# Turning the head stacks of Q and K two heads at a time, with the third part written by a DMA within SBUF

## The reference

```python
x = x + 0.5 * ffn(_layernorm(x), w_gate, w_up, w_down)
x = x + attn(_layernorm(x), w_qkv, w_out, q_gain)
x = x + 0.5 * ffn(_layernorm(x), w_gate, w_up, w_down)

def ffn(x, w_gate, w_up, w_down):        # hidden size 2048
    return (silu(x @ w_gate.T) * (x @ w_up.T)) @ w_down.T

def attn(x, w_qkv, w_out, q_gain):
    q, k, v = split(x @ w_qkv)           # 16 heads of 32
    q, k = unit_norm(q), unit_norm(k)    # t * rsqrt(sum(t * t) + 1e-6)
    q, k = rope(q), rope(k)              # in every second head
    logits = (q @ k.T) * q_gain          # causal mask
    return (softmax(logits) @ v) @ w_out
```

## Time and profile before

| | |
|---|---|
| median of 3 runs | 2797.44 us (2796.15 to 2797.51) |
| the profiled execution | 2798.85 us |
| its span, first to last instruction | 2797.1 us |
| mean granted clock of PE | 0.994 |
| PE busy | 2726.2 us (97%) |
| DVE busy | 1780.7 us (64%) |
| ACT busy | 1205.0 us (43%) |
| POOL busy | 531.2 us (19%) |

### The profile page before, as it was taken

The page is one execution under the profiler, slowest core; times in us unless marked ns, Lnnn a source line. Parts: engine busy times, 40 slices in busy tenths (PEclk is TensorE's granted clock), DMA queues, the critical chain, the costliest instruction groups (busy, mean ns, idle before and its releaser), DMA issues.

```text
span 2797.1 us, 56089 instructions
## 1 busy us (share of the span) xinstructions
PE 2726.2 (97%) x22720; PEld 1992.9 (71%) x22720; DVE 1780.7 (64%) x5054; ACT 1205.0 (43%) x2250; POOL 531.2 (19%) x820
## 2 busy tenths in 40 slices
PE   4999999999999999999999999999999999999999
PEld 4677766777767777777767777677777776777776
DVE  7766666666656565666656666565666767676643
ACT  5443544354434434443434445344443444454422
POOL 0012132213130302213121121312203131313100
PEclk8999999999999999999999999999999999999999
DMA  7000000000000000000000000000000000000000
GB/s 257 1 16 1 16 1 1 1 17 16 2 1 16 16 2 1 1 16 16 2 1 9 9 16 1 1 16 9 8 5 13 16 2 1 1 16 9 2 9 16
DMA packets 16577, 39.37 MB, mean 14 GB/s; under 512 B 1472, under 2 KB 1472, under 8 KB 15808
## 3 DMA queue, kind: packets, MB, share of 16 engines
q1 hardware_dynamic: 16320, 35.79, 3.6%
HBM read 26.35 MB, written 9.44 MB: 13 GB/s over the span
## 4 chain that ended last, share of the span: by engine, by line
PE 87%; DVE 8%; issue 3%; ACT 2%; DMA 0%; POOL 0%; SPq 0%; DVEq 0%; ACTq 0%
PE psum L1045 25%; PE psum L1046 25%; PE psum L1047 25%; PE psum L1200 2%; PE psum L1176 2%; PE psum L1212 2%; PE psum L1068 1%; PE psum L1154 1%; PE psum L1158 1%; DVE arena L885 1%; DVE arena L883 1%; DVE arena L960 1%; PE psum L1213 1%; DVE arena L889 1%; ACT arena L775 1%
## 5 line engine op out<-in xcount | busy, mean ns | idle before, releaser
L1045 PE MATMUL psum<-arena,WG 128*128 128x256 f16 x2048 | 558.8, 273 | 4.9 <-DVE arena L885 3.4
L1045 PE MATMUL psum<-arena,WU 128*128 128x256 f16 x2048 | 558.9, 273 | 0.0
L1047 PE MATMUL psum<-arena,WG 128*128 128x256 f16 x2048 | 558.7, 273 | 0.0
L1047 PE MATMUL psum<-arena,WU 128*128 128x256 f16 x2048 | 558.5, 273 | 0.0
L1046 PE MATMUL psum<-arena,WU 128*128 128x256 f16 x2048 | 558.5, 273 | 0.0
L1046 PE MATMUL psum<-arena,WG 128*128 128x256 f16 x2048 | 558.5, 273 | 0.0
L883 DVE SCALAR_TENSOR_TENSOR arena<-arena,psum 128x256 f32<-128x256 f32 x512 | 214.8, 420 | 446.2 <-ACT arena L775 445.2
L775 ACT ACTIVATE arena<-psum,tscale 128x256 f32<-128x256 f32 x512 | 241.1, 471 | 564.4 <-PE psum L1047 563.7
L1045 PE MATMUL psum<-WD,arena 128*128 128x512 f16 x1024 | 388.8, 380 | 3.6 <-DVE arena L889 3.5
L1047 PE MATMUL psum<-WD,arena 128*128 128x512 f16 x1024 | 388.4, 379 | 0.0
L1046 PE MATMUL psum<-WD,arena 128*128 128x512 f16 x1024 | 388.4, 379 | 0.0
(11 more groups left out here) (145 smaller groups left out, 4465.2 us busy)
## 6 DMA issues: line engine op xcount, KB each, us to landing
arena<-in_L_attn_x SPq DMA_DIRECT2D x16, 512.0 KB, 3.7
out<-arena SPq DMA_DIRECT2D x16, 512.0 KB, 2.8
arena<-in_L_ffn_w_gate SPq DMA_DIRECT2D x4, 1024.0 KB, 9.2
arena<-in_L_ffn_w_up SPq DMA_DIRECT2D x4, 1024.0 KB, 7.3
WD<-in_L_ffn_w_down SPq DMA_DIRECT2D x4, 1024.0 KB, 12.5
arena<-in_L_attn_w_qkv SPq DMA_DIRECT2D x1, 3072.0 KB, 22.2
arena<-in_L_attn_w_out SPq DMA_DIRECT2D x1, 1024.0 KB, 6.7
park<-arena SPq DMA_DIRECT2D x2, 512.0 KB, 2.8
```

The source lines that it names most:

```text
L1045: T_.matmul(o, lhs(0), rhs(0), start=first, stop=False)
L1047: return T_.matmul(o, lhs(1), rhs(0), start=False, stop=last)
```

## The change

The stacks of Q and K are laid out as two parts for each head, 64 columns, in place of three: high, low for Q and low, high for K. The parts of two heads are then 128 adjacent columns, and one transpose turns them (`stk`, four for Q and four for K in place of eight and eight). The even head comes out on partitions 0 to 63 of PSUM, the odd one on 64 to 127 (`turned_pair`). ACT and DVE bring each with an own copy to partitions 0 to 63 of `QT` and `KT`. The third part, partitions 64 to 95, equals the first of Q (high) and the second of K (high), and SP copies it within SBUF with one DMA each (`stack_high`), which waits for the copy of this tile. The first score product of a half batch waits for the DMAs (`qt_dup`, `kt_dup`) in place of the copies. ACT writes all high parts of a tile in one activation where there were three. The order has a new stage "stack high" and a new `fill` "dup" behind the last tile, and shares of both tables are set anew.

```diff
@@ -103,7 +103,10 @@
     qn = [words("work", 2 * D + D * i, D) for i in range(2)]
     ropeU = words("work", 4 * D, D // 2)
     ropeV = words("work", 4 * D + D // 2, D // 2)
-    STK = halves("work", 5 * D, HH * ST).rearrange("p (h c) -> p h c", h=2 * HH)
+
+    stk = halves("work", 5 * D, (2 * D + 2 * HD) // 2)
+    STQ, STK = (stk[:, D * a:D * (a + 1)].rearrange("p (h c) -> p h c", h=HH) for a in range(2))
+    SThi = stk.rearrange("p (a c) -> p a c", a=2)[:, :, 0:D].rearrange("p a (h c) -> p a h c", c=2 * HD)[:, :, :, 0:HD]
 
     fH = [words("ffn", TH * i, TH) for i in range(2)]
     HP = [[halves("ffn", 2 * TH + TH * q + TH // 2 * i, TH // 2) for q in range(2)] for i in range(2)]
@@ -171,6 +174,10 @@
     def ps16(b):
         return psum[:, b * 512:(b + 1) * 512].bitcast(F16)
 
+    def turned_pair(bank, odd):
+
+        return ps16(bank)[2 * HD * odd:2 * HD * (odd + 1), 0:D].rearrange("p (h n) -> p h n", n=P)
+
     def wd_bank(m):
         return (0, 1, 2, 6, 7)[m % 5]
 
@@ -185,7 +192,7 @@
         dn_tr dn_st gmax_in gmax_all scales wd_hi wd_lo sel_done pro_hi pro_lo dve_pro pool_pro
         x_in0 x_in1 stored0 stored1 x1_done x2_done out_ready var_ready rstd_ready xn_done xt_ps xt_hi xt_lo
         qk_ps v_ps qs_done sq_done vhi_done vlo_done ssq_ready r_ready qn_done rope_done
-        st_hi st_lo qt_ps kt_ps qt_ev kt_ev s1_ps smax_done mst_done mt_ps mt_copied mrow_done
+        st_hi st_lo qt_ps kt_ps qt_ev kt_ev qt_dup kt_dup s1_ps smax_done mst_done mt_ps mt_copied mrow_done
         s2_ps exp_done cut_done phi_done plo_done pv_ps y_read ynorm_done yt_ps yt_hi yt_lo op_ps
         gu_ps tanh_done a_done gated h_hi h_lo down_done dve_chain pool_chain"""
     s = {n: nc.alloc_semaphore(n) for n in names.split()}
@@ -346,9 +353,10 @@
                 if t:
                     put(("stack", b, hf, t - 1))
                     fill(w["stack"])
-                    bank3(("stack turn", b, hf, t - 1), ("stack out", b, hf, t - 1))
+                    bank3(("stack turn", b, hf, t - 1), ("stack out", b, hf, t - 1), ("stack high", b, hf, t - 1))
                 else:
                     fill(w["v first"])
+            fill(w["dup"])
             fill(w["turned"])
 
         def maxima(b, hf, h, w):
@@ -471,12 +479,14 @@
 
     LOAD, LEFT, PACE = 9, 3, (0, 2, 3, 4)
     SHORT = (0, 1, 6, 7)
-    MANY = {"qk": 1.88, "qk first": 1, "ends": 3, "stack": 2, "v first": 1.25, "turned": 1, "max first": 0.4,
+    MANY = {"qk": 1.32, "qk first": 1, "ends": 1.92, "stack": 2, "v first": 1.25, "turned": 1, "max first": 0.4,
             "maxima": 1, "max rows": 1, "scores": 1, "exp": 1.5, "high": 1, "low": 1, "max": 1,
-            "head": 1, "end": 1, "end values": 0.5, "out 0": 1, "out 1": 2, "out 2": 1, "out 3": 1}
-    FEW = {"qk": 1, "qk first": 2, "ends": 2.4, "stack": 2, "v first": 1, "turned": 1, "max first": 0.32,
-           "maxima": 1, "max rows": 1, "scores": 0.8, "exp": 1.2, "high": 0.8, "low": 0.8, "max": 0.56,
-           "head": 0.56, "end": 0.8, "end values": 1, "out 0": 1.25, "out 1": 1.25, "out 2": 1, "out 3": 1.5}
+            "head": 1, "end": 1, "end values": 0.5, "out 0": 1, "out 1": 2, "out 2": 1.5, "out 3": 1,
+            "dup": 3}
+    FEW = {"qk": 1, "qk first": 2, "ends": 2.4, "stack": 2, "v first": 1.5, "turned": 1, "max first": 0.32,
+           "maxima": 1, "max rows": 0.8, "scores": 0.8, "exp": 1.2, "high": 0.8, "low": 0.8, "max": 0.56,
+           "head": 0.56, "end": 0.8, "end values": 1, "out 0": 1.25, "out 1": 1.25, "out 2": 1, "out 3": 1.5,
+           "dup": 3}
     ORDER = order()
     norms = [stage[1:] for stage in ORDER if stage[0] == "norm"]
     place_of_norm = {norm: k for k, norm in enumerate(norms)}
@@ -580,7 +590,15 @@
                 p, half = at
                 sp.dma_start(X[p][:, 2 * half:2 * half + 2, :], of).then_inc(s[loaded(what)[0]], 16)
 
-            run({"store": store, "load": load})
+            def stack_high(b, hf, t):
+
+                c = slice(t * P, (t + 1) * P)
+                sp.wait_ge(s["qt_ev"], tile_no(b, hf, t) + 1)
+                sp.dma_start(QT[2 * HD:ST, :, c], QT[0:HD, :, c]).then_inc(s["qt_dup"], 16)
+                sp.wait_ge(s["kt_ev"], tile_no(b, hf, t) + 1)
+                sp.dma_start(KT[2 * HD:ST, :, c], KT[HD:2 * HD, :, c]).then_inc(s["kt_dup"], 16)
+
+            run({"store": store, "load": load, "stack high": stack_high})
             for th in range(2):
                 sp.wait_ge(s[f"stored{th}"], 16 * len(STORES[th]))
 
@@ -736,14 +754,13 @@
                 if t:
                     act.wait_ge(s["kt_ps"], i)
                 q3 = qn[t % 2].rearrange("p (h c) -> p h c", c=HD)
-                nc.scalar.activation(STK[:, :, 0:HD], q3, ACT.Copy)
-                nc.scalar.activation(STK[:, 0:HH, HD:2 * HD], q3[:, 0:HH, :], ACT.Copy)
-                nc.scalar.activation(STK[:, HH:2 * HH, 2 * HD:ST], q3[:, HH:2 * HH, :], ACT.Copy).then_inc(s["st_hi"], 1)
+                nc.scalar.activation(SThi, q3.rearrange("p (a h) c -> p a h c", a=2), ACT.Copy).then_inc(s["st_hi"], 1)
 
             def stack_out(b, hf, t):
                 act.wait_ge(s["qt_ps"], tile_no(b, hf, t) + 1)
-                nc.scalar.activation(QT[0:ST, :, t * P:(t + 1) * P], ps16(2)[0:ST, :].rearrange("p (h n) -> p h n", h=HH),
-                                     ACT.Copy).then_inc(s["qt_ev"], 1)
+                for odd in range(2):
+                    ins = nc.scalar.activation(QT[0:2 * HD, odd::2, t * P:(t + 1) * P], turned_pair(2, odd), ACT.Copy)
+                ins.then_inc(s["qt_ev"], 1)
 
             def max_rows(b, hf, g):
                 act.wait_ge(s["mt_ps"], group_no(b, hf, g) + 1)
@@ -919,12 +936,14 @@
             def stack(b, hf, t):
                 dve.wait_ge(s["st_hi"], tile_no(b, hf, t) + 1)
                 q3 = qn[t % 2].rearrange("p (h c) -> p h c", c=HD)
-                V_.tensor_tensor(STK[:, 0:HH, 2 * HD:ST], q3[:, 0:HH, :], STK[:, 0:HH, 0:HD], ALU.subtract)
-                V_.tensor_tensor(STK[:, HH:2 * HH, HD:2 * HD], q3[:, HH:2 * HH, :], STK[:, HH:2 * HH, 0:HD], ALU.subtract).then_inc(s["st_lo"], 1)
+                V_.tensor_tensor(STQ[:, :, HD:2 * HD], q3[:, 0:HH, :], STQ[:, :, 0:HD], ALU.subtract)
+                V_.tensor_tensor(STK[:, :, 0:HD], q3[:, HH:2 * HH, :], STK[:, :, HD:2 * HD], ALU.subtract).then_inc(s["st_lo"], 1)
 
             def stack_out(b, hf, t):
                 dve.wait_ge(s["kt_ps"], tile_no(b, hf, t) + 1)
-                V_.tensor_copy(KT[0:ST, :, t * P:(t + 1) * P], ps16(3)[0:ST, :].rearrange("p (h n) -> p h n", h=HH)).then_inc(s["kt_ev"], 1)
+                for odd in range(2):
+                    ins = V_.tensor_copy(KT[0:2 * HD, odd::2, t * P:(t + 1) * P], turned_pair(3, odd))
+                ins.then_inc(s["kt_ev"], 1)
 
             mnegv = mneg[:, :].rearrange("p (t h) -> p t h", t=TT)
             mstv = mst[:, :].rearrange("p (t h c) -> p t h c", t=TT, c=2)
@@ -1150,12 +1169,12 @@
                 i = tile_no(b, hf, t)
                 pe.wait_ge(s["st_lo"], i + 1)
                 take(2, "qt_ev", i + 1)
-                for h in range(HH):
-                    ins = T_.transpose(ps16(2)[0:ST, h * P:(h + 1) * P], STK[:, h, :], ident16[:, :])
+                for m in range(HH // 2):
+                    ins = T_.transpose(ps16(2)[:, m * P:(m + 1) * P], stk[:, m * P:(m + 1) * P], ident16[:, :])
                 ins.then_inc(s["qt_ps"], 1)
                 take(3, "kt_ev", i + 1)
-                for h in range(HH):
-                    ins = T_.transpose(ps16(3)[0:ST, h * P:(h + 1) * P], STK[:, HH + h, :], ident16[:, :])
+                for m in range(HH // 2):
+                    ins = T_.transpose(ps16(3)[:, m * P:(m + 1) * P], stk[:, D + m * P:D + (m + 1) * P], ident16[:, :])
                 ins.then_inc(s["kt_ps"], 1)
 
             def bank_free(bank):
@@ -1166,8 +1185,8 @@
 
             def scores_max(b, hf, h):
                 if h == 0:
-                    pe.wait_ge(s["qt_ev"], tile_no(b, hf, TT))
-                    pe.wait_ge(s["kt_ev"], tile_no(b, hf, TT))
+                    pe.wait_ge(s["qt_dup"], 16 * tile_no(b, hf, TT))
+                    pe.wait_ge(s["kt_dup"], 16 * tile_no(b, hf, TT))
                     scored[0] = None
                 for bank, tiles in enumerate(QBANKS):
                     bank_free(bank)
```

## The result

The changed kernel takes 2767.53 us (median of 4 runs, 2767.09 to 2768.96) against 2797.48 for the kernel before, measured beside it: a ratio of 0.9893, 95% interval 0.9877 to 0.9909, or 30.0 us less. The forecast was 2773, 24.5 us less. The span went from 2797.1 to 2765.7.

The account below looks back on a forecast made before the run. PE's stream was taken to bound the kernel, busy 97%. Transposes -28.7, "max rows" +2.7, other lost cover +1.5, transfers 0 sum to -24.5 us: 2773 us from a median of 2797.44, range 2763 to 2788.

Parts of the forecast that it names:

- The transposes: PE's stack turns: eight fewer transposes in each of 64 tiles, 56 ns apiece, saving 28.7 us.
- ACT and DVE: Around the turn: ACT's high parts 820 ns shorter, copies 159 (ACT) and 163 ns (DVE) longer; counted as nothing.
- The transfers: Copies within SBUF before each half batch's first score product: land before PE arrives, cost 0, kept at 0 to 6 us.
- The slower rival: Transfers within SBUF land too late; at 7 us each half waits 3.4 us, 2827 us in all; chance 0.07.
- The shares of the short batches: Cover moved to the new wait thins other places in the short batches: 2.7 us plus 1.5 us lost.
- "max rows" at 0.8: Short batches, between transposed maxima and first score product: cover sometimes nothing, PE waits for ACT's copy, 2.7 us.
- The middle batches' shorter fills: Middle batches, last tile's unit step to its turn: cover falls from 7.3 to 5.6 pieces, costing nothing.

Follow-up runs that it names:

- "dup" 1: Changed kernel with the fill behind the last stack turn cut from 3 shares to 1 and "ends" two shares more in both tables: 2792.57 us, ratio 0.9984.
- the old shares: Changed kernel with both share tables as before and only the one piece of "turned" between last stack turn and first score product: 2826.18 us, ratio 1.0105.
- the run head by head: Changed kernel with each head turned by itself, 8 + 8 transposes of 64 columns a tile, one 64x1024 copy each for Q and K: 2805.19 us, ratio 1.0027.

## Why the prediction was right

**The transposes: right in mechanism and size.** 0.45 us a tile less, 28.7 us, is seen in the timeline. The run with each transpose twice gives 25.6 of it back in time. The loads of 128 columns are the quicker ones, as the value products suggested: 110 ns for 64 columns, 123 for 96, 98 for 128. The Trainium skill (TensorE: Matmul & The Clock Gate, section LDWEIGHTS) gives a load's time as its columns over 1.2 GHz, as an estimate 53, 80 and 107 ns for these three; the traces disagree for 64 and 96.

**ACT and DVE: right.** Estimated 589 and 425 ns a copy, measured 592 and 421. ACT's relief was counted as nothing; it is worth 2 to 3 us, since the new shares made the turns wait for the stacks.

**The transfers: right, with a smaller margin.** 2.1 us to land, where 2.3 to 3.7 were taken. The estimate by the fit of the Trainium skill (DMA: Bandwidth & Descriptors, Anatomy of one DMA), which is given there for DMAs that GpSimd issues, was 2.2, and these, issued by SP, agree with it. With runs of 256 bytes they take no longer than the fit says; no run here has the same transfer in longer runs. But SP needs 0.6 us for an issue, not 0.38, so they are there at 4.5 us after the first transpose, 1.2 before PE. The slower rival had the right mechanism: with too little cover the kernel is 29 us slower than before. Its threshold of 24.5 us in waits, 1.5 us a half, is borne out: with "dup" 1 PE stands 21 us and 25.0 of the 30.0 us are lost. Beyond it its price was too low: it had 2827 for waits of 3.4 us a half, and the old shares came to 2826.18 with 2.7, since most of those waits lowered the clock as well.

**The shares of the short batches: the step that failed.** "max rows" at 0.8 was to cost 2.7 us by a wait for ACT's copy, and 1.5 us more elsewhere. A wait of that size did come at the second pass (2.0 us in five places in the matmul queue), but the profile names DVE's row maxima for it, and giving the share back, together with "v first", removed neither it nor any time. Against these new waits of PE (second pass and stack turn) stand shorter ones for the maxima, and the two tables on the old kernel measure the same within 0.1%. The term should have been nothing. That is 4.2 of the 5.5 us by which the forecast was too high. By the runs, the change is then made up of 25.6 (transposes, by the run with twice as many) to 28.7 us (by their distance), 2.6 for ACT and nothing that can be told for the shares: 28.2 to 31.3, against 30.0 measured.

**The middle batches' shorter fills: nearly right.** They were put at nothing. Of the four turns that wait for the stacks none lies in batches 2 to 5.

## What to carry to other kernels

Where one engine's stream is 97% of the time, count starts, not busy times: what is removed from the stream comes off the total nearly one for one, and the rest is a question of whether each new result arrives before that engine does. A transfer that is moved off the engine must be bought with cover at the place where it is awaited, here 4 us of other work, and the margin must include the issue time of a second transfer in the same queue. When pieces are dealt out by rounded shares, compare two settings only with the pieces of all other places held; one share given to "ends" or to all places moved the time by 13 us, most of it through where the pieces fall.

## What the runs showed of the hardware that was not expected

- Waits of PE of 2.4 to 2.7 us were followed by a granted clock of 0.50 over some 3 us in 11 of 16 halves; waits of 1.0 to 1.4 us in none. The length of the wait alone doesn't decide it: with 2.7 us the clock fell in 8 of 13, with 2.4 in all three. The kernel before has a wait ending at 151.41 with 2.8 us between starts, and a clock of 0.57 from 151 to 155; the changed kernel has one of the same length there and 1.00.
- Transposes with 64-column weights, eight and eight between wider matmuls, lose 0.09 us at the start of a turn and 0.11 within and behind it; those with 96 and 128 columns lose nothing. Why is open: between the run head by head and the one with each transpose twice only the loads' width and the copies behind the turn differ.
- A DMA within SBUF of 32 partitions in 256-byte runs, 64 KB, lands in 2.1 us (at most 3.6 in the changed kernel), but holds SP's queue for 0.6 us, where a store of 512 KB in runs of 2 KB held it 0.38.
